# Second half of the value projection in another PSUM bank, second norm turned in its place

## The reference, cut to what matters

```
h  = gat(gat(x, adj, W1, a1), adj, W2, a2)
h  = ln(x + h)                                   # norm 0
x1 = ln(h + relu(h @ w_ff1 + b) @ w_ff2 + b)     # norm 1
out = sum over r of (softmax(q k^T / sqrt(32)) * (adj == r)) @ (x1 @ Wv[r] + bv[r]),  r = 0..3
x2 = ln(x1 + out @ Wo + bo)                      # norm 2
y  = ln(x2 + gelu(x2 @ W1 + b) @ W2 + b)         # norm 3
```

## Time and profile before

| | |
|---|---|
| median of three runs | 3147.11 us |
| the profiled execution: its own time | 3145.98 us |
| the profiled execution: span from first to last instruction | 3144.2 us |
| mean granted TensorE clock over the span | 0.988 |
| busy: TensorE matmuls, weight loads | 97%, 87% |
| busy: VectorE, ScalarE, GpSimd | 71%, 77%, 60% |

### The profile page before, as it was taken

How to read it: one execution, slowest core, us unless ns; L and a number is a source line. 1 busy time by engine, 2 the same in 40 slices (tenths; PEclk the granted TensorE clock), 3 DMA queues, 4 the chain that set the end, 5 groups by cost and what they waited for, 6 DMA issues and landing times.

```text
span 3144.2 us, 78504 instructions
## 1 busy us (share of the span) xinstructions
PE 3034.5 (97%) x26980; PEld 2739.5 (87%) x26980; DVE 2228.3 (71%) x4975; ACT 2434.3 (77%) x6218; POOL 1876.3 (60%) x1747
## 2 busy tenths in 40 slices
PE   5799999999999999999999999999999999999997
PEld 4788888888888888888888889889889889889885
DVE  4677777677777777777777777777777777777763
ACT  3578878878878878878778778788787787787774
POOL 3365665665665665665665665665666666666663
PEclk7899999999999999999999999999999999999998
DMA  3000100100100100100100100100100100100100
GB/s 143 25 22 24 33 27 23 33 27 23 33 27 23 33 27 23 33 27 23 33 27 23 33 27 23 33 27 23 33 27 23 33 27 23 33 27 23 33 12 14
DMA packets 101943, 93.54 MB, mean 30 GB/s; under 512 B 14736, under 2 KB 101008, under 8 KB 101776
## 3 DMA queue, kind: packets, MB, share of 16 engines
q1 hardware_dynamic: 101904, 93.00, 9.6%
HBM read 76.17 MB, written 16.78 MB: 30 GB/s over the span
## 4 chain that ended last, share of the span: by engine, by line
PE 90%; DVE 7%; ACT 1%; issue 1%; POOL 0%; DVEq 0%; DMA 0%; POOLq 0%; SPq 0%; ACTq 0%
PE ps_f L290 11%; PE ps_f L292 10%; PE ps_f L291 10%; PE ps_ao L487 7%; PE ps L477 6%; PE ps L290 5%; PE ps L291 5%; PE ps L292 5%; PE ps L467 4%; PE ps_ao L290 4%; PE ps_ao L532 4%; PE ps_g L291 3%; PE ps_g L290 3%; PE ps_g L292 3%; PE ps_ao L291 3%; PE ps_ao L292 3%
## 5 line engine op out<-in xcount | busy, mean ns | idle before, releaser
L1026 POOL TENSOR_TENSOR hid_lo<-hid_full,hid_hi 128x512 fp32r<-128x512 f32 x512 | 672.4, 1313 | 409.7 <-ACT hid_hi L648 390.6
L290 PE MATMUL ps_f<-down_w_hi,hid_hi 128*128 128x256 f32 x2048 | 592.9, 290 | 1.3 <-POOL hid_lo L1026 1.3
L1003 POOL TENSOR_TENSOR rstd<-vareps,neg_half 128x2 f32<-128x2 f32 x256 | 218.2, 852 | 610.7 <-DVE vareps L821 610.7
L291 PE MATMUL ps_f<-down_w_lo,hid_hi 128*128 128x256 f32 x2048 | 575.1, 281 | 0.0
L292 PE MATMUL ps_f<-down_w_hi,hid_lo 128*128 128x256 f32 x2048 | 574.8, 281 | 0.0
L665 ACT ACTIVATE prob<-ps,s_least 128x256 f32<-128x256 f32 x1024 | 469.4, 489 | 6.0 <-DVE s_least L869 5.2
L869 DVE TENSOR_REDUCE s_least<-ps 128x4 f32<-128x1024 f32 x256 | 309.4, 1209 | 140.4 <-PE ps L467 140.3
L290 PEld LDWEIGHTS ps_f<-down_w_hi,hid_hi 128*128 128x128 f32 x2048 | 385.6, 188 | 23.4 <-issue 19.9
L292 PEld LDWEIGHTS ps_f<-down_w_hi,hid_lo 128*128 128x128 f32 x2048 | 392.3, 192 | 0.0
L291 PEld LDWEIGHTS ps_f<-down_w_lo,hid_hi 128*128 128x128 f32 x2048 | 386.1, 189 | 0.0
L648 ACT ACTIVATE hid_hi<-hid_full 128x512 fp32r<-128x512 f32 x512 | 323.7, 632 | 16.3
(11 more groups left out here) (158 smaller groups left out, 9447.0 us busy)
## 6 DMA issues: line engine op xcount, KB each, us to landing
adj_in<-adj_keys SPq DMA_DIRECT2D x128, 256.0 KB, 2.9
xT_in<-x_features SPq DMA_DIRECT2D x64, 256.0 KB, 2.7
norm<-x_nodes SPq DMA_DIRECT2D x64, 256.0 KB, 2.7
out_nodes<-norm SPq DMA_DIRECT2D x64, 256.0 KB, 2.1
row_vectors<-all_row_vectors SPq DMA_DIRECT2D x1, 1536.0 KB, 10.4
raw_up<-L_w_ff SPq DMA_DIRECT2D x1, 1024.0 KB, 9.5
raw_down<-L_w_ff SPq DMA_DIRECT2D x1, 1024.0 KB, 11.7
raw_v<-L_Wv SPq DMA_DIRECT2D x4, 256.0 KB, 8.9
```

The costliest lines, as they stand in the source:

```text
L290: nc.tensor.matmul(ps_out, left[0], right[0], start=first, stop=False)
L291: nc.tensor.matmul(ps_out, left[0], right[1], start=False, stop=False)
L1026: pool.tensor_tensor(hid[1][:, 2 * m:2 * m + 2, :], hid_full[:, 2 * m:2 * m + 2, :], value(hid[0][:, 2 * m:2 * m + 2, :]), ALU.subtract).t ...
```

## The change

The second half of the values (parts 1 and 3 of `V_PARTS`, nodes 128 to 255) is written to `ps_f` in place of `ps_ao`; the turned norm 1 is written to `ps_ao` in place of `ps_f`. The waits follow the banks: `pe_v(b, 1)` waits for `ysum[1](a, 1)` (norm 1's sum has read `ps_f`) and no more for `v_set(b, 1)`; `pe_turn(a, 1)` waits in addition for `v_set(b, 1)`; `pe_av_all(b, 0)` waits in addition for `hT_lo[1](a, 1)`, the last reader of the turned norm; `pe_up(d, 1, 2)` waits for the values' readers and no more for the turned norm's. On VectorE, `dve_turned(a, 1)` moves ahead of the branch `dve_mask_more(b, 0)`. Nothing is added to or taken from the computation.

```diff
-        turn_bank = [ps_g[:, 1, :], ps_f[:, 0, :], ps_ao[:, 0, :]]
+        turn_bank = [ps_g[:, 1, :], ps_ao[:, 0, :], ps_ao[:, 0, :]]
 
         def pe_turn(pe, g, n):
             pe.wait_ge(*norm_set[n](g, 2))
+            if n == 1 and (not isinstance(g, int) or g > 0):
+                pe.wait_ge(*v_set(g - 1, 1))
...
             if l == 1 and m == 2:
-                if not isinstance(g, int) or g < B - 2:
-                    pe.wait_ge(*hT_lo[1](g + 2, 1))
+                if not isinstance(g, int) or g < B - 1:
+                    pe.wait_ge(*v_set(g + 1, 2))
+                    pe.wait_ge(*v_more_set(g + 1, 2))
                 elif g > 0:
                     pe.wait_ge(*ysum[3](g - 1, 1))
...
+        v_bank = [ps_ao[:, 0, :], ps_f[:, 0, :]]
+
         def v_product(g, n):
             j, rr = V_PARTS[n]
             for k in range(C):
-                last = product(ps_ao[:, 0, :], cut(hT[1], k, nodes(j)), cut(v_w, k, slice(rr * 512, rr * 512 + 512)),
+                last = product(v_bank[j], cut(hT[1], k, nodes(j)), cut(v_w, k, slice(rr * 512, rr * 512 + 512)),
                                k == 0, k == C - 1)
...
             if n:
-                pe.wait_ge(*v_set(g, n))
+                if not isinstance(g, int) or g < B - 1:
+                    pe.wait_ge(*ysum[1](g + 1, 1))
+                elif g > 1:
+                    pe.wait_ge(*ysum[3](g - 2, 1))
...
                 for n in range(2):
-                    pe.wait_ge(*(v_more_set(g, 1) if n else v_set(g, 2)))
+                    pe.wait_ge(*v_set(g, n + 1))
                     v_product(g, 2 + n).then_inc(v_more_done.sem, 1)
+                pe.wait_ge(*v_more_set(g, 1))
...
             if hg == 0:
                 pe.wait_ge(*v_set(g, 2))
                 pe.wait_ge(*v_more_set(g, 2))
+                if not isinstance(g, int) or g < B - 1:
+                    pe.wait_ge(*hT_lo[1](g + 1, 1))
...
         def v_out(n):
             j, rr = V_PARTS[n]
-            return nc.vector.tensor_tensor(v_sb[:, j, rr * 512:(rr + 1) * 512], ps_ao[:, 0, :],
+            return nc.vector.tensor_tensor(v_sb[:, j, rr * 512:(rr + 1) * 512], v_bank[j],
                                            v_bias[:, rr * 512:(rr + 1) * 512], ALU.add)
...
                 dve_flag(dve, b)
                 dve_v_more(dve, b)
+            if ff0:
+                dve_turned(dve, a, 1)
+            if att1:
                 dve_mask_more(dve, b, 0)
-            if ff0:
-                dve_turned(dve, a, 1)
```

More of the change, by code:

```diff
@@ L948, in dve_body @@
                 dve_v_more(dve, b)
-                dve_mask_more(dve, b, 0)
             if ff0:
                 dve_turned(dve, a, 1)
+            if att1:
+                dve_mask_more(dve, b, 0)
             if gat:
```

## The result

The kernel after takes 3114.78 us, the median of four runs (3113.41 to 3115.58), against 3146.95 us for the kernel before in the same set of runs. The ratio is 0.99, with a 95% interval of 0.9886 to 0.9914. The change makes the kernel faster by 32 us.

What follows compares the result with a forecast made beforehand. TensorE was taken as the bound, busy 987.64 of 1000 us. Sixty bodies at 0.195 us (11.7) plus 1.1 us in bodies 61 and 62 took 12.8 us off 3145.98; with the median 1.1 above, 3134.3 us, 80% range 3124 to 3150.

Steps and rivals of the forecast that it cites:

- The wait that goes: Second value product no longer waits for VectorE's emptying of the first half; it starts 0.76 us sooner a body.
- The turn meets its input: Turn of norm 1 now waits 0.18 us for ScalarE's second norm instruction, leaving 0.58 of the 0.76 us.
- The new wait at the attention product: `rec_wide` transposes wait for `hT_lo`, which starts 0.45 us sooner; TensorE's gain shrinks from 0.76 to 0.25 us a body.
- refill: First matmul after the attention product's wait may cost up to 0.11 us more; gain 0.14 to 0.25, taken as 0.195.
- The branch that moves: On VectorE, one flag branch instead of two ahead of `dve_turned`, hidden by the 0.68 us emptying: costs nothing.
- The rival of an uncovered branch: VectorE's branch isn't hidden, so `hT_lo` starts late: 11 to 18 us slower, 3158 to 3165 us; chance 0.11.
- VectorE's reduction gets out of GpSimd's way: Rival: VectorE's second reduction and GpSimd's affine step swap order; 0.35 us a body, 22 us, 3125 us; chance 0.08.
- the other waits: Remaining waits in the body, such as `pe_up(d, 1, 2)` and the mask fence, cost nothing; the rest moves with TensorE.
- the wait that I called the loss: TensorE's wait for `v_sb` at the second value product, priced at 0.76 us a body.

Runs made afterwards that it cites:

- a_waitlast: Kernel after, with the attention product's wait for `hT_lo` moved behind that for `rec_wide`, as last of four: 3115.92 us, ratio 0.9911.
- a_vwait: Kernel after, with the removed wait of the second value product for `v_set` of the first half put back, banks still changed: 3145.52 us, ratio 1.0014.
- a_novmove: Kernel after, with VectorE's old order, the second branch on the flag ahead of `hT_lo` again: 3111.79 us, ratio 0.99.
- b_stall: Kernel before with its own banks, plus a wait of the attention product for `hT_lo`, not needed there: 3144.72 us, ratio 0.9998.
- b_drain: Kernel before, plus a wait ahead of the first attention product for TensorE's own last up projection matmul: 3141.15 us, ratio 0.9987.
- b_drain_late: Kernel before, plus a wait for TensorE's own last matmul behind the first attention product, straight ahead of the long string: 3126.81 us, ratio 0.9942.
- b_wait2: Kernel before, plus an always met wait for `v_set` ahead of layer 1's third up projection: 3141.14 us, ratio 0.9993.
- a_wait1: Kernel after, without the redundant wait for `v_set` ahead of layer 1's third up projection: 3112.81 us, ratio 0.9906.
- a_up1first: Kernel after, with `pe_up(d, 1, 1)`, twelve matmuls, moved ahead of the first attention product: 3099.6 us, ratio 0.9852.
- a_up1_drain: Kernel after, with `pe_up(d, 1, 1)` moved ahead of the attention product and a wait for TensorE's own last matmul between them: 3123.12 us, ratio 0.9926.

## Why the prediction was wrong in size

The direction and the chain were right, point by point:

- *The wait that goes.* The second value product comes 0.83 us sooner; 0.76 was forecast. The eight transposes ahead of it take 1524.84 - 1524.05 = 0.79 us when the product follows at once, not the 0.87 read from the second string of them.
- *The turn meets its input.* It waits 0.16 us for ScalarE's norm, against 0.18, and starts 0.51 us sooner, against 0.58: it goes on 0.14 us after the norm, where 0.06 was taken.
- *The new wait at the attention product.* `hT_lo` follows `v_sb` without a gap (0.62 us from start to start) and starts 0.46 us sooner, against 0.45. Here the size was off: the step had TensorE go on 0.06 us after `hT_lo`, the release of the value product's wait. It took 0.26, and with the order of the waits turned 0.15 (a_waitlast). That a met wait stands behind the late one doesn't explain it alone: the value product of a_vwait has two waits in that order and starts 1540.13 - (1539.42 + 0.66) = 0.05 us after `v_sb`, and the turn, also with two, took the 0.14 above. So a release measured at one place didn't hold at another; why is open. The direct gain is then 0.06 us at the transposes and 0.03 at the string, not 0.25 less a refill. With only this corrected, the forecast would have been 60 x 0.03 to 0.06, or 2 to 4 us and under one more in bodies 61 and 62: no change.
- *The branch that moves.* Nothing, as forecast, and a_novmove shows it even with two. The rival of an uncovered branch would have given a gap ahead of `hT_lo`; there is none. The Trainium skill (Advanced Engine Details and Errata, Control Flow Timing) puts a compare and branch at about 0.108 us; two of them under 0.68 us fit that, while a stall like the loop turn's 0.41 us for each would not have.
- *VectorE's reduction gets out of GpSimd's way.* It takes 1.48 us, not 0.4, and starts behind GpSimd's step as before. This rival did not happen; its time of 3125 is nearest to the result by accident.

**The step that failed** is the last sentence of the other waits: "All else in the body hangs on TensorE and moves with it." It hangs on TensorE, but TensorE's own pace is not a constant of the program. I took the rest of the body as 47.30 us less what its head gains. In fact the head's new wait turned 94 steps of 117.7 ns into 113.3, 0.41 us, and with the two other strings that changed pace it is 0.45 of the 0.48 us. The two errors have opposite signs: 0.17 us too much at the head (0.195 against 0.03), 0.45 too little behind it.

What caused the gain can be told in two ways, and both are measured. From before to b_stall or a_vwait the new wait costs 0.4 us and its pace gives 0.4 back (period 47.30 to 47.27); from a_vwait to after, taking away the wait for `v_sb` gives 0.46 us a body directly. In that order the wait that I called the loss is worth nearly all the gain, and the new wait nothing. The new wait alone doesn't show in the time of the kernel before (b_stall); the other bank alone, without the new wait, can't be had, since the turned norm must have left the bank.

**Shown:** the string of 96 has two paces at the same granted clock. A halt of TensorE at the transposes brings the 113 ns pace, whatever it waits for and whichever banks are used: all 60 bodies have it in the kernel after, in b_stall and in b_drain, where the transposes start 0.52 us behind the matmul ahead of them. So does a halt at the string (b_drain_late, all 60). A redundant wait that is met anyway does not (b_wait2, none of 60), nor does its removal take the pace away (a_wait1, all 60). The pace, once taken, holds to the end of the string. The halt is neither always enough nor the only way: with the shorter one of a_waitlast 42 bodies of 60 have the pace, and in a_up1first, with none there, 10 of 60.

**Open:** what in the string's start picks it. From the last matmul of the attention product on, the steps into and through the string's start, in the bodies shown, are 309, 226, 114, 119, 117 and 118 ns in the kernel before, and 309, 223, 119, 116, 114 and 113 in the kernel after. The second of these, from the string's first matmul to its second, tells the two apart in this string of all fourteen kernels traced here (bodies 1 to 60 of each, 840 strings): it is 225 or 226 ns in the 250 strings of the upper pace and 220 to 224 ns in the 590 of the lower. So the pace is settled when the second matmul starts, by a difference of a few ns whose source no run isolates. The string of 34 behind the turn of norm 2 runs at 117.8 ns in the kernels before and after, but not everywhere: in b_drain 28 of 55 bodies have 113.3 ns there. Whether a halt ahead of that string or of the one behind the score products pays was not tried.

The Trainium skill (Perfetto Trace Analysis, Tensor Engine Instruction) warns that the end of a matmul is an estimate of the profiler. The trace agrees: records of 0.28 us stand 0.113 or 0.118 us apart, so the lengths don't give the pace, though their mean moves with it (276 and 281 ns).

## What to carry to other kernels

Where TensorE is the bound, measure its pace from start to start, string by string, before and after a change: 4 ns on a matmul of 113 ns is 4% of a string's time, and no wait shows it. A wait taken off the head of a body is worth what the last of the waits behind it lets through, so follow the chain to the next long string. Price the release after a wait by a row at the same place of the body where there is one; from another place it was 0.06 us here for 0.26. When a kernel has a long string at the higher of two paces, one cheap wait on TensorE's own last result ahead of it is worth a trial (19 us of 3146 here); ahead of short transposes such a wait cost 0.4 to 0.5 us and took back the gain.

## What the runs showed of the hardware that was not expected

- Two paces, 113.3 and 117.7 ns from start to start, for the same string of 128 x 256 matmuls with 128 x 128 weights, at a granted clock of 1.00 for both. At that clock of 2.4 GHz the 4.4 ns are 10.6 cycles a matmul. The string (84 matmuls where one part of the up projection was moved) takes one of them within its first five steps and keeps it to its end, and the step from its first matmul to its second already tells which: 220 to 224 ns for the lower, 225 or 226 for the upper, in 840 of 840 strings.
- A wait for TensorE's own last matmul costs 0.16 to 0.17 us of matmul time ahead of a string, but 0.40 us ahead of the transposes of `rec_wide` and 0.51 in a_up1_drain.
- How soon TensorE goes on after what it waited for differs by place: 0.26 us at the transposes of `rec_wide`, 0.15 there with that wait as the last of four (a_waitlast), 0.14 at the turn, and 0.05 at the value product of a_vwait, though two waits stand ahead of it.
- Adding a wait can make a kernel faster: b_drain_late, 0.9942 (0.9924 to 0.996).
